# A gated graph network on one core: the first layer's two products in the other order

## The chip, the cores and the metric

The kernel runs on one core of one Trainium2 chip. The core has TensorE (PE: matmuls, with its weight loads shown apart as PEld), VectorE (DVE), ScalarE (ACT), GpSimd (POOL) and SyncE (SP), which issues all DMA transfers of this kernel. The metric is the time of one execution in device microseconds, as the median of the runs.

## The reference

There are 128 graphs of 128 nodes with 256 features, and one adjacency matrix for all of them. A first layer computes `norm(x + adj x W0 + b0)`; a gated recurrent network with three steps follows, then a residual and another norm.

```python
y = jnp.einsum('nm,bmd->bnd', adj, x)                  # first layer
x = _layernorm(x + jnp.einsum('bnd,do->bno', y, weight) + bias)
h = x
for _ in range(3):
    a = jnp.einsum('nm,bmd->bnd', adj, h)              # in_mat = out_mat = adj
    av = jnp.concatenate([a, a], axis=-1)
    z = sigmoid(_lin(av, w3_w, w3_b) + _lin(h, u3_w, u3_b))
    r = sigmoid(_lin(av, w4_w, w4_b) + _lin(h, u3_w, u3_b))
    hv = jnp.tanh(_lin(av, w5_w, w5_b) + _lin(r * h, u5_w, u5_b))
    h = (1.0 - z) * h + z * hv
out = _layernorm(x + h)
```

All of it is float32.

## The kernel before

**Tiling.** Four graphs make a group (1024 float32 values in each of 128 partitions); there are 32 groups. One step of one group is a *slot*; there are 96 slots. `at(s)` says which group and step slot s is: four groups advance in turn, so of 12 slots the first four are step 0 of four groups, the next four step 1, the last four step 2. The DVE work differs: in slots s with s mod 12 from 1 to 8 the state just updated must be turned (`state_blocks`, L881); in s mod 12 = 9, 10, 11, 0 it is not. The text calls these *heavy* and *light* slots.

**Split products.** A float32 operand is split in a high part (an fp32r copy, made by ACT, `copy`) and a low part (full minus high, made by DVE, `low_part`, L745). A product is then three fp32r matmuls, hi·hi, lo·hi and hi·lo, that accumulate in PSUM. So every operand of PE costs one ACT and one DVE pass of 128x1024.

**A slot on PE** (L537 to L546): `graph(s+1)` (adjacency times the next slot's state, L447, 6 matmuls of 512 columns), `state_product(s)` (12, L379), then `first_layer(s)` if there is any, `r_product` (12), `candidate_product` (12), `gates` (24). The text takes the beginning of `graph(s+1)` as the beginning of slot s.

**The graph result's way.** The adjacency product is by nodes; the gates want features in the partitions. DVE turns 32x32 blocks of it (`graph_blocks`, L826, two operations of 512), SP writes them to DRAM (`write_a`) and reads them back with the quadrants exchanged (`read_a`, four DMAs), ACT makes `a_hi` from what landed and DVE `a_lo`. The same trip by DRAM is made by the state (`state_blocks`, `write_h`, `read_h`) and by the first layer's result (`first_blocks`, `write_h0`, `read_h0`).

**The first layer** of groups 4 to 31 is spread over the slots of earlier groups, one group per three slots, by `GRAPH, WEIGHTS, NORM = -12, -10, -9`. In a slot with s mod 3 = 0 PE does `first_graph` (L402: 8 float32 matmuls of 128 columns with x itself as the weights, which the profile counts as 16); ACT and DVE split the result (`ax_hi`, `ax_lo`). In the slot two later (s mod 3 = 2) PE does `first_weights` (L413: 24 matmuls of 256 columns) and DVE `first_sum` (L788, and statistics). In the next one (s mod 3 = 0 again) ACT does `first_norm` and DVE `first_blocks`. POOL adds the bias to x (`add_bias`, L1014) once `first_graph` is done, and computes scale and shift. An output group is finished in slots with s mod 3 = 1 (`residual` on DVE, L815, with statistics) and 2 (`result_norm` on ACT). The text speaks of slots of kind 0, 1 and 2, by s mod 3.

**Order.** There is no scheduler: each engine runs the loop `for s in range(END + 1)` in the order written, and waits on semaphores. What stands behind a waiting instruction on its engine waits too. Among the waits: `state_product(s+1)` needs both halves of z of slot s (`z_ready`), since they share PSUM banks; `gates(s)` ends with the `u5` product, which needs `rh_hi` (ACT) and `rh_lo` (DVE) of this slot.

Of the kernel before, what the change touches and what calls it, by code (L numbers as in the profile page):

```python
# [11 lines left out]
G = 4  # L12
C = 2
Q = 32
# [5 lines left out]
def gnn_kernel(nc, x, adj_t, w0, b0, w3_t, w4_t, w5_t, u3_t, u5_t, biases, out):  # L20
# [31 lines left out]
    def group_at(s, offset):  # L52

        g, rest = divmod(s - offset, STEPS)
        return g if rest == 0 and FOUR <= g < GROUPS else None

    def graph_at(s):

        return FOUR if s == 1 else group_at(s, GRAPH) if s > 0 else None
# [8 lines left out]
    GRAPH, WEIGHTS, NORM = -12, -10, -9  # L68
# [16 lines left out]
    with ExitStack() as ctx:  # L85
# [56 lines left out]
        h0_scratch = scratch("h0_scratch")  # L142
# [18 lines left out]
        def by_node(ps):  # L161
            return ps[:, :, :].rearrange("p c (b d) -> p (c b) d", d=D)

# [31 lines left out]
        x_half = sem("x_half")  # L195
        x_loaded, out_stored = some(X_RING, sem, "x_loaded"), some(2, sem, "out_stored")
# [44 lines left out]
        def _(sp):  # L241
# [70 lines left out]

            def store_last():
# [24 lines left out]
            load(4)  # L338

            for s in range(END + 1):  # L340
                h0_next = group_at(s, NORM + 1) if s + 1 >= FOUR else s + 1
# [29 lines left out]
        def _(pe):  # L371
# [13 lines left out]
            def first_graph(g, batches=range(G)):  # L385
# [7 lines left out]
                if g >= FOUR:  # L393
                    pe.wait_ge(y_added, after(g - 1))
# [11 lines left out]
            def first_weights(g, batches=range(G)):  # L406
                banks, (hi, lo) = first_banks(g), first_parts(g)
                pe.wait_ge(ax_lo_ready, after(g) if batches[-1] == G - 1 else 1)
                for b in batches:
                    for c in range(C):  # L410
                        cols = slice(b * N, (b + 1) * N)
                        for n, (v, w) in enumerate(((hi, w0_hi), (hi, w0_lo), (lo, w0_hi))):
                            mm = pe.matmul(by_node(banks)[:, b, :], v[:, c, cols], w[:, c, :],  # L413
                                           start=n == 0 and c == 0, stop=n == 2 and c == C - 1,
                                           skip_group_check=True)
                mm.then_inc(y_done, 1)
# [141 lines left out]
        def _(act):  # L558
# [9 lines left out]
            def first_graph_high(g):  # L568
                hi, _ = first_parts(g)
                act.wait_ge(ax_done, after(g))  # L570
                if g >= FOUR:
                    act.wait_ge(y_done, after(g - 1))
                elif g >= 2:
                    act.wait_ge(y_done, after(g - 2))
                copy(hi[:, :, :], first_banks(g)[:, :, :]).then_inc(ax_hi_ready, 1)

# [45 lines left out]
            def node_high(s):  # L622
# [12 lines left out]
                copy(in_quadrants(nat_hi), chunks_first(src)).then_inc(nat_hi_ready, 1)  # L635
# [74 lines left out]
            for s in range(END + 1):  # L710
# [6 lines left out]
                if (g := graph_at(s)) is not None:  # L717
                    first_graph_high(g)
# [18 lines left out]
                if s < SLOTS:  # L737
                    update_gate(s)
                    candidate(s, 0)


        @block.vector
        def _(dve):
# [39 lines left out]

            def first_sum(g):
# [7 lines left out]
            def first_blocks(g):  # L792
                dve.wait_ge(h0_ready, g + 1)
                if g >= 1:
                    dve.wait_ge(h0_written, g * 16)
                if g < FOUR:
# [23 lines left out]
            def graph_blocks(s):  # L820
# [4 lines left out]
                for c in range(C):  # L825
                    tr = dve.transpose(a_blocks[:, :, c, :].rearrange("p i (b e) -> p i b e", e=Q),  # L826
                                       ps_a[:, c, :].rearrange("p (i b f) -> p i b f", b=G, f=Q))
                tr.then_inc(a_blocks_ready, 1)

            def node_low(s):  # L830
# [3 lines left out]
                low_part(in_quadrants(nat_lo), chunks_first(src), in_quadrants(nat_hi)).then_inc(nat_lo_ready, 1)  # L834
# [126 lines left out]
            for s in range(END + 1):  # L961
# [26 lines left out]
                if (g := graph_at(s)) is not None:  # L988
# [14 lines left out]
        def _(pool):  # L1003
# [6 lines left out]
            def add_bias(g):  # L1010
                pool.wait_ge(ax_done, after(g))
# [48 lines left out]
            for s in range(END + 1):  # L1060
# [3 lines left out]
                if (g := graph_at(s)) is not None:  # L1064
                    add_bias(g)
                if (g := group_at(s, WEIGHTS)) is not None:
# [37 lines left out]
```

## Time and profile before

| | us |
|---|---|
| median of 3 runs | 1620.86 (1619.14 to 1620.9) |
| the profiled execution | 1620.69 |
| its span | 1618.9 |
| PE busy | 1599.5 (99%) |
| DVE busy | 1427.4 (88%) |
| ACT busy | 940.4 (58%) |
| POOL busy | 265.6 (16%) |
| DMA | 268.26 MB, queue busy 52.9% |

Busy time is the time in which at least one instruction of the engine ran. Matmuls overlap each other, so one matmul's duration says little; the chain of waits, in which each piece begins where the one before it ends, tells what a group of matmuls costs. TensorE's granted clock was full (1.00) in the stretches that are used below. In a timeline the bracket behind a row is the idle time ahead of it and who ended it.

### The profile page before, as it was taken

To read this page: it belongs to the slowest core of one execution; us is meant where nothing else is said; L and a number is where in the kernel's file an instruction comes from. 1 tells how busy PE (TensorE), PEld (TensorE's weight loads), DVE (VectorE), ACT (ScalarE), POOL (GpSimd) and SP (SyncE) were. 2 spreads that over 40 slices of the span, in tenths; PEclk is the share of its full clock that TensorE was granted. 3 is DMA by queue.
4 is the path that set the end of the run, shared out by engine and by line. 5 is a ranking of instruction groups with operands and counts; after the bars stand their busy time and mean duration, and the time that the engine had idled before them with its cause. 6 is when DMAs were issued, how large, how long until landed. Compare 5 with 4: busy or idle time off the path is not lost.

```text
span 1618.9 us, 21710 instructions
## 1 busy us (share of the span) xinstructions
PE 1599.5 (99%) x7684; PEld 1348.8 (83%) x7684; DVE 1427.4 (88%) x1904; ACT 940.4 (58%) x1364; POOL 265.6 (16%) x302
## 2 busy tenths in 40 slices
PE   8999999999999999999999999999999999999996
PEld 8888888888888888888888888888888888888875
DVE  6788888999889998998889988999988999888888
ACT  4556556565555666565665556565656555556554
POOL 5111111111111111101111111111011111100022
PEclk9999999999999999999999999999999999999998
DMA  5444345664456553666526664355644566556534
GB/s 158 140 157 147 127 140 173 196 204 151 127 169 208 185 168 104 183 207 196 169 102 185 191 212 144 125 187 176 214 143 136 178 195 183 156 146 201 177 127 143
DMA packets 195596, 268.26 MB, mean 166 GB/s; under 512 B 18976, under 2 KB 167456, under 8 KB 195488
## 3 DMA queue, kind: packets, MB, share of 16 engines
q1 hardware_dynamic: 195488, 266.88, 52.9%
q8 instruction: 61, 1.00, 0.3%
q14 instruction: 47, 0.39, 0.1%
HBM read 135.21 MB, written 131.60 MB: 165 GB/s over the span
## 4 chain that ended last, share of the span: by engine, by line
PE 93%; DVE 3%; DMA 1%; SPq 1%; ACT 0%; issue 0%; POOL 0%; ACTq 0%; DVEq 0%; POOLq 0%
PE ps_r L379 46%; PE ps_h L379 31%; PE ps_a L447 8%; PE ps_l L413 5%; PE ps_l L402 3%; SPq L259 1%; DMA bias_row<-b 0%; PE ps_a L428 0%; DMA h_scratch_a<-h_blocks_a 0%; DVE out_sums L750 0%; DVE a_blocks L826 0%; DVE nat_lo L745 0%; DVE hv L866 0%; DMA a_landed<-a_scratch_b 0%; DVE h_t_h L873 0%
## 5 line engine op out<-in xcount | busy, mean ns | idle before, releaser
L826 DVE STREAM_TRANSPOSE a_blocks<-ps_a 128x512 f32<-128x512 f32 x184 | 120.0, 690 | 81.8 <-PE ps_a L447 81.5
L666 ACT ACTIVATE rh<-ps_r,bias_r 128x512 f32<-128x512 f32 x192 | 131.1, 688 | 104.2 <-PE ps_r L379 100.8
L560 ACT ACTIVATE rh_hi<-rh 128x512 fp32r<-128x512 f32 x192 | 119.0, 633 | 107.2 <-DVE rh L854 106.6
L682 ACT ACTIVATE hv<-ps_h,bias_h 128x512 f32<-128x512 f32 x192 | 128.9, 686 | 43.1 <-PE ps_h L379 42.5
L1022 POOL TENSOR_TENSOR out_var_eps_sb<-out_meanvar,eps 128x4 f32<-128x4 f32 x31 | 7.4, 239 | 808.6 <-DVE out_meanvar L756 808.6
L745 DVE TENSOR_TENSOR rh_lo<-rh,rh_hi 128x512 fp32r<-128x512 f32 x192 | 125.8, 689 | 9.2
L866 DVE TENSOR_TENSOR hv<-hv,z_sb 128x1024 f32<-128x1024 f32 x95 | 116.5, 1226 | 11.0 <-DVE hv L863 1.4
L678 ACT ACTIVATE z_sb<-ps_r,bias_z 128x512 f32<-128x512 f32 x192 | 119.9, 672 | 4.4 <-PE ps_r L379 4.4
L560 ACT ACTIVATE nat_hi<-h_landed_a 128x1024 fp32r<-128x1024 f32 x39 | 41.4, 1062 | 139.4 <-DMA h_landed_a<-h_scratch_a 129.4
L379 PE MATMUL ps_h<-rh_hi,u_hi 128*128 128x512 f32 x384 | 119.1, 391 | 1.6 <-ACT rh_hi L560 1.5
L379 PE MATMUL ps_r<-a_hi_a,w_hi 128*128 128x512 f32 x384 | 119.9, 393 | 0.6 <-ACT rh L666 0.6
L379 PE MATMUL ps_r<-a_hi_b,w_hi 128*128 128x512 f32 x384 | 119.8, 393 | 0.0
L379 PE MATMUL ps_h<-rh_lo,u_hi 128*128 128x512 f32 x384 | 118.7, 390 | 0.0
L379 PE MATMUL ps_h<-rh_hi,u_lo 128*128 128x512 f32 x384 | 118.7, 390 | 0.0
L379 PE MATMUL ps_r<-h_hi,u_hi 128*128 128x512 f32 x384 | 118.5, 390 | 0.0
L379 PE MATMUL ps_r<-a_hi_a,w_lo 128*128 128x512 f32 x384 | 118.4, 389 | 0.0
L379 PE MATMUL ps_r<-a_hi_b,w_lo 128*128 128x512 f32 x384 | 118.4, 389 | 0.0
L379 PE MATMUL ps_r<-h_lo,u_hi 128*128 128x512 f32 x384 | 118.3, 389 | 0.0
L379 PE MATMUL ps_r<-a_lo_a,w_hi 128*128 128x512 f32 x384 | 118.3, 389 | 0.0
L379 PE MATMUL ps_r<-a_lo_b,w_hi 128*128 128x512 f32 x384 | 118.3, 389 | 0.0
L379 PE MATMUL ps_r<-h_hi,u_lo 128*128 128x512 f32 x384 | 118.2, 389 | 0.0
L379 PEld LDWEIGHTS ps_h<-rh_hi,u_hi 128*128 128x128 f32 x384 | 72.2, 188 | 17.3 <-ACT rh_hi L560 2.4
(291 smaller groups left out, 4006.6 us busy)
## 6 DMA issues: line engine op xcount, KB each, us to landing
h_scratch_a<-h_blocks_a SPq DMA_DIRECT2D x48, 512.0 KB, 5.3
h_landed_a<-h_scratch_a SPq DMA_DIRECT2D x192, 128.0 KB, 2.9
h_scratch_b<-h_blocks_b SPq DMA_DIRECT2D x47, 512.0 KB, 3.5
h_landed_b<-h_scratch_b SPq DMA_DIRECT2D x188, 128.0 KB, 2.9
a_scratch_a<-a_blocks SPq DMA_DIRECT2D x46, 512.0 KB, 2.6
a_landed<-a_scratch_a SPq DMA_DIRECT2D x184, 128.0 KB, 2.9
a_scratch_b<-a_blocks SPq DMA_DIRECT2D x46, 512.0 KB, 2.7
a_landed<-a_scratch_b SPq DMA_DIRECT2D x184, 128.0 KB, 2.8
```

What stands on the lines that cost most here:

```text
L259: sp.dma_start(landed[to * Q:(to + 1) * Q].rearrange("q i c x -> q i (c x)"), by_target[to]).then_inc(moved, 16)
L379: mm = pe.matmul(psum[:, o, :], w[:, c, o * P:(o + 1) * P], v[:, c, :], start=start and n == 0 and c == 0, stop=stop and n == 2 and c == C ...
L402: mm = pe.matmul(into, x_in[g % X_RING][:, b, c * P:(c + 1) * P], adjt[:, :], start=True, stop=True)
L413: mm = pe.matmul(by_node(banks)[:, b, :], v[:, c, cols], w[:, c, :], start=n == 0 and c == 0, stop=n == 2 and c == C - 1, skip_group_check ...
L447: mm = pe.matmul(ps_a[:, c, :], w[:, :], v[:, c, :], start=k == 0, stop=k == 2, skip_group_check=True)
L560: return act.activation(dst, src, ACT.Copy)
L666: act.activation(rh[:, c, :], ps_r[:, c, :], ACT.Sigmoid, bias=bias_r[:, c:c + 1]).then_inc(r_ready, 1)
L678: act.activation(z_sb[:, c, :], ps_r[:, c, :], ACT.Sigmoid, bias=bias_z[:, c:c + 1]).then_inc(z_ready, 1)
L682: act.activation(hv[:, c, :], ps_h[:, c, :], ACT.Tanh, bias=bias_h[:, c:c + 1]).then_inc(hv_ready, 1)
L745: return dve.tensor_tensor(dst, full, hi.bitcast(F32), ALU.subtract)
L826: tr = dve.transpose(a_blocks[:, :, c, :].rearrange("p i (b e) -> p i b e", e=Q), ps_a[:, c, :].rearrange("p (i b f) -> p i b f", b=G, f=Q))
L866: dve.tensor_tensor(hv[:, :, :], hv[:, :, :], z_sb[:, :, :], ALU.mult).then_inc(scaled_ready, 1)
```

## The change

**What PE computes.** For groups 4 to 31 the first layer is adjacency times (x W0) and no longer (adjacency times x) W0. `first_product(g)` is 24 fp32r matmuls of 256 columns with the turned x as weights, `graph_of_product(g)` 6 fp32r matmuls of 512 columns with the split adjacency as weights. Groups 0 to 3 stay as they were.

**How x is turned.** x W0 wants features in the partitions. DVE turns x in 32x32 blocks (`turn`), SP writes them to a new DRAM tensor (`write_x`) and reads them back into the buffer `h_t` of that group, which is free then (`read_x`). ACT and DVE split it (`turned_high`, `turned_low`) and split the product as well (`product_high`, `product_low`).

**When.** The table gives `TURN` = 3g-14 (kind 1), `PRODUCT` = 3g-11 (kind 1), `SUM` = 3g-10 (kind 2), `NORM` = 3g-9 (kind 0). Group 4 has numbers of its own. The load of x moves from kind 1 to kind 2, two slots ahead of `TURN`. POOL's `add_bias` waits for `turn` and no longer for PE.

**Graph result.** `nat_hi` and `nat_lo` are filled flat, in the order of their source, so that the graph result can be turned in one operation of 1024.

```diff
-    GRAPH, WEIGHTS, NORM = -12, -10, -9
+    LATER = range(FOUR, GROUPS)
+    TURN = {g: 0 if g == FOUR else STEPS * g - 14 for g in LATER}
+    PRODUCT = {g: 2 if g == FOUR else STEPS * g - 11 for g in LATER}
+    SUM = {g: PRODUCT[g] + 1 for g in LATER}
+    NORM = {g: PRODUCT[g] + 2 for g in LATER}
+    BLOCKS_AT = {g: 5 if g == FOUR else NORM[g] for g in LATER}
...
                 if FOUR <= s + 1 < SLOTS:
                     write_a(s + 1)
                 if h0_next is not None:
                     write_h0(h0_next)
+                if x_next is not None:
+                    write_x(x_next)
...
                     read_h0(h0_next)
+                if x_next is not None:
+                    read_x(x_next)
...
-                if (g := group_at(s, GRAPH - 2)) is not None and g > FOUR:
+                if (g := group_at(s, TURN, -2)) is not None and g >= FOUR + 2:
                     load(g)
...
+            def first_product(g):
+                pe.wait_ge(y_added, after(g - 1))
+                pe.wait_ge(xt_lo_ready, g - FOUR + 1)
...
+            def graph_of_product(g):
+                pe.wait_ge(xw_lo_ready, g - FOUR + 1)
+                for half in range(C):
+                    for k, (w, v) in enumerate(((adj_hi, ax_hi), (adj_lo, ax_hi), (adj_hi, ax_lo))):
+                        mm = pe.matmul(ps_l[:, half, :], w[:, :], v[:, half, :], start=k == 0, stop=k == 2,
...
             def first_layer(s):
-                if (g := graph_at(s)) is not None:
-                    first_graph(g)
-                if (g := group_at(s, WEIGHTS)) is not None:
-                    first_weights(g)
+                if (g := group_at(s, PRODUCT)) is not None:
+                    first_product(g)
+                if (g := group_at(s, SUM)) is not None:
+                    graph_of_product(g)
...
+            def turned_high(g):
+                act.wait_ge(y_done, after(g - 1))
+                act.wait_ge(x_moved, (g - FOUR + 1) * MOVED)
...
+            def product_high(g):
+                act.wait_ge(xw_done, g - FOUR + 1)
+                copy(flat(ax_hi), flat(ps_l)).then_inc(xw_hi_ready, 1)
...
-                for c in range(C):
-                    tr = dve.transpose(a_blocks[:, :, c, :].rearrange("p i (b e) -> p i b e", e=Q),
-                                       ps_a[:, c, :].rearrange("p (i b f) -> p i b f", b=G, f=Q))
+                tr = dve.transpose(flat_blocks(a_blocks).rearrange("p (x e) -> p x e", e=Q),
+                                   flat(ps_a).rearrange("p (x f) -> p x f", f=Q))
...
-                if (g := graph_at(s)) is not None:
-                    first_graph_low(g)
-                if (g := group_at(s, WEIGHTS)) is not None:
+                if (g := group_at(s, PRODUCT)) is not None:
+                    product_low(g)
+                if (g := group_at(s, SUM)) is not None:
                     first_sum(g)
-                if (g := group_at(s, NORM)) is not None:
+                if (g := group_at(s, BLOCKS_AT)) is not None:
                     first_blocks(g)
+                if (g := group_at(s, TURN)) is not None:
+                    turn(g)
+                if (g := group_at(s, PRODUCT, -1)) is not None:
+                    turned_low(g)
...
-                pool.wait_ge(ax_done, after(g))
+                if g < FOUR:
+                    pool.wait_ge(ax_done, after(g))
+                else:
+                    pool.wait_ge(x_blocks_ready, g - FOUR + 1)
```

POOL's order stays as it is: `first_scale` of one group (its last operation is `h_shift`, L1028), and then `add_bias` of the next. The names `ax_hi`, `ax_lo` serve the turned x and the product in turn. `h_blocks` stands for the buffers of the first layer (`h0_blocks`) and of the state alike. Three places where the order of instructions changes. DVE, slot 43 (kind 1), from the graph result's low part to the end; before:

```order
570 L745 TENSOR_TENSOR a_lo_a<-a_landed,a_hi_a 128x1024
571 L815 TENSOR_TENSOR h_nat_d<-h_nat_d,h_landed_b 128x1024
572 L750 BN_STATS out_sums<-h_nat_d 128x6 x4
573 L756 BN_AGGR out_meanvar<-out_sums 128x2 x4
574 L826 STREAM_TRANSPOSE a_blocks<-ps_a 128x4x128 x2
```

and of the changed kernel:

```order
599 L822 TENSOR_TENSOR a_lo_a<-a_landed,a_hi_a 128x1024
600 L822 TENSOR_TENSOR ax_lo<-ps_l,ax_hi 128x1024
601 L869 STREAM_TRANSPOSE h_blocks<-x_in_d 128x8x4x32
602 L918 TENSOR_TENSOR h_nat_d<-h_nat_d,h_landed_b 128x1024
603 L827 BN_STATS out_sums<-h_nat_d 128x6 x4
604 L833 BN_AGGR out_meanvar<-out_sums 128x2 x4
605 L930 STREAM_TRANSPOSE a_blocks<-ps_a 128x1024
```

Two operations, the product's low part and the turning of x, now stand between the graph result's low part and the residual, and the turning of the graph result is one operation. DVE, the end of slot 42 (kind 0), before:

```order
557 L745 TENSOR_TENSOR h_lo<-h_t_h,h_hi 128x1024
558 L745 TENSOR_TENSOR a_lo_b<-a_landed,a_hi_b 128x1024
559 L745 TENSOR_TENSOR ax_lo<-ps_l,ax_hi 128x1024
560 L802 STREAM_TRANSPOSE h_blocks<-h_nat_b 128x1024
561 L826 STREAM_TRANSPOSE a_blocks<-ps_a 128x4x128 x2
```

and of the changed kernel:

```order
586 L822 TENSOR_TENSOR h_lo<-h_t_h,h_hi 128x1024
587 L822 TENSOR_TENSOR a_lo_b<-a_landed,a_hi_b 128x1024
588 L905 STREAM_TRANSPOSE h_blocks<-h_nat_b 128x1024
589 L822 TENSOR_TENSOR ax_lo<-h_t_c,ax_hi 128x4x8x32
590 L930 STREAM_TRANSPOSE a_blocks<-ps_a 128x1024
```

Here the count stays: the low part of the graph product makes room for that of the turned x (`ax_lo<-h_t_c`). SP's DMA queue around a slot of kind 2, before:

```order
355 L259 DMA h_landed_a<-h_scratch_a 32x4x256 x4
356 L254 DMA a_scratch_a<-a_blocks 128x1024
357 L259 DMA a_landed<-a_scratch_a 32x4x256 x4
358 L254 DMA h_scratch_b<-h_blocks_b 128x1024
359 L259 DMA h_landed_b<-h_scratch_b 32x4x256 x4
```

and of the changed kernel:

```order
255 L283 DMA h_landed_a<-h_scratch_a 32x4x256 x4
256 L278 DMA a_scratch_a<-a_blocks 128x1024
257 L278 DMA x_scratch<-h_blocks 128x1024
258 L283 DMA a_landed<-a_scratch_a 32x4x256 x4
259 L283 DMA h_t_c<-x_scratch 32x4x256 x4
260 L275 DMA x_in_d<-x 128x4x256
261 L278 DMA h_scratch_b<-h_blocks_b 128x1024
262 L283 DMA h_landed_b<-h_scratch_b 32x4x256 x4
```

The write of x stands between the write and the read of the graph result, and the read of x and the load of another group ahead of the state's write.

## Rows read from the trace of the kernel before

**Rows 1.** The page: busy time and share of the span of each engine.

```profile
span 1618.9 us, 21710 instructions
PE 1599.5 (99%) x7684; PEld 1348.8 (83%) x7684; DVE 1427.4 (88%) x1904; ACT 940.4 (58%) x1364; POOL 265.6 (16%) x302
```

**Rows 2.** Waits of PE, the largest: for whom, us in total, times, longest.

```profile
PE ps_l L413 <- DVE nat_lo L745: 3.4, 1, 3.4
```

**Rows 3.** The chain of waits, slots 41 to 43: start, us, what.

```profile
710.26 1.36 PE ps_a L447 x6
...
714.34 2.87 PE ps_l L413 x24
...
728.12 1.36 PE ps_a L447 x6
...
732.20 1.78 PE ps_l L402 x16
...
744.88 1.36 PE ps_a L447 x6
```

**Rows 4.** Timeline of DVE, slots 40 to 43 and 45: start, us, operation.

```profile
708.47 1.23 DVE L745 TENSOR_TENSOR a_lo_b<-a_landed,a_hi_b 128x1024 fp32r<-128x1024 f32 x1 [0.65 <-ACT a_hi_b L560]
...
712.67 1.28 DVE L826 STREAM_TRANSPOSE a_blocks<-ps_a 128x512 f32<-128x512 f32 x2
...
729.52 1.31 DVE L826 STREAM_TRANSPOSE a_blocks<-ps_a 128x512 f32<-128x512 f32 x2 [1.23 <-PE ps_a L447]
...
734.56 1.25 DVE L881 STREAM_TRANSPOSE h_blocks_a<-h_t_f 128x1024 f32<-128x1024 f32 x1
735.73 1.20 DVE L881 STREAM_TRANSPOSE h_blocks_b<-h_t_d 128x1024 f32<-128x1024 f32 x1
736.86 1.18 DVE L745 TENSOR_TENSOR nat_lo<-h_landed_b,nat_hi 128x1024 fp32r<-128x1024 f32 x1
737.96 1.28 DVE L854 TENSOR_TENSOR rh<-rh,h_t_g 128x512 f32<-128x512 f32 x2
...
742.82 1.22 DVE L745 TENSOR_TENSOR ax_lo<-ps_l,ax_hi 128x1024 fp32r<-128x1024 f32 x1
743.96 1.24 DVE L802 STREAM_TRANSPOSE h_blocks<-h_nat_b 128x1024 f32<-128x1024 f32 x1
746.28 1.31 DVE L826 STREAM_TRANSPOSE a_blocks<-ps_a 128x512 f32<-128x512 f32 x2 [1.09 <-PE ps_a L447]
...
785.31 2.15 DVE L745 TENSOR_TENSOR nat_lo<-h_landed_b,nat_hi 128x1024 fp32r<-128x1024 f32 x1
```

**Rows 5.** Timeline of ACT, slots 40 to 44, the same columns.

```profile
722.91 1.06 ACT L560 ACTIVATE a_hi_a<-a_landed 128x1024 fp32r<-128x1024 f32 x1 [0.83 <-DMA a_landed<-a_scratch_a]
...
739.81 1.05 ACT L560 ACTIVATE a_hi_b<-a_landed 128x1024 fp32r<-128x1024 f32 x1
...
742.74 1.24 ACT L678 ACTIVATE z_sb<-ps_r,bias_z 128x512 f32<-128x512 f32 x2
...
757.31 1.06 ACT L560 ACTIVATE a_hi_a<-a_landed 128x1024 fp32r<-128x1024 f32 x1 [1.76 <-DMA a_landed<-a_scratch_a]
```

**Rows 6.** Timeline of POOL, slots 42 and 45.

```profile
730.01 0.20 POOL L1028 TENSOR_TENSOR h_shift<-h_mean_rstd,minus_one 128x4 f32<-128x4 f32 x1
...
781.66 1.24 POOL L1028 TENSOR_TENSOR h_shift<-h_mean_rstd,minus_one 128x4 f32<-128x4 f32 x1
783.65 2.72 POOL L1014 TENSOR_TENSOR x_in_d<-x_in_d,bias_row 128x1024 f32<-128x1024 f32 x1 [0.74 <-PE ps_l L402]
```

**Rows 7.** Timeline of SP's DMA queue, slot 44 (issues).

```profile
764.19 0.34 SPq L254 DMA_DIRECT2D a_scratch_b<-a_blocks  x1
769.27 1.73 SPq L259 DMA_DIRECT2D a_landed<-a_scratch_b  x4
```

**Rows 8.** Stretches: slots 40 and 41 (kinds 1, 2); the last columns are clock, DMA share, GB/s.

```profile
695.30:710.26 14.96, 14.96 (x68) 12.39 (x67) 12.96 (x15) 8.22 (x11) 0.00 (x0) 1.00 0.81 222
710.26:728.12 17.86, 17.86 (x92) 15.26 (x91) 17.21 (x30) 9.92 (x15) 3.38 (x4) 1.00 0.53 176
```

More of the change, by code:

```diff
@@ L50, in output_slot, with group_at, turned_in_a_blocks @@
         return slot_of(g, STEPS - 1) + 1 + (0 if g >= GROUPS - FOUR else 2 * (g % FOUR))
[L52 to L59, printed above, removed]
+    LATER = range(FOUR, GROUPS)
[4 more added lines that the diff above has]
+    BLOCKS_AT = {g: 5 if g == FOUR else NORM[g] for g in LATER}
+    def group_at(s, stage, behind=0):
+        for g in LATER:
+            if stage[g] + behind == s:
+                return g
+        return None
+    def turned_in_a_blocks(g):
+        return g < FOUR + 2
     def after(g):
@@ L338, in _ @@
             load(4)
+            load(5)
             for s in range(END + 1):
-                h0_next = group_at(s, NORM + 1) if s + 1 >= FOUR else s + 1
+                h0_next = group_at(s, BLOCKS_AT, 1) if s + 1 >= FOUR else s + 1
+                x_next = group_at(s, TURN, 1)
                 if FOUR <= s + 1 < SLOTS:
@@ L415, in first_weights @@
                                            skip_group_check=True)
+                mm.then_inc(y_done, 1)
+            def first_product(g):
+                pe.wait_ge(y_added, after(g - 1))
+                pe.wait_ge(xt_lo_ready, g - FOUR + 1)
+                hi, lo = by_batch_and_chunk(ax_hi), by_batch_and_chunk(ax_lo)
+                for b in range(G):
+                    for c in range(C):
+                        for n, (v, w) in enumerate(((hi, w0_hi), (hi, w0_lo), (lo, w0_hi))):
+                            mm = pe.matmul(by_node(ps_l)[:, b, :], v[:, b * C + c, :], w[:, c, :],
+                                           start=n == 0 and c == 0, stop=n == 2 and c == C - 1,
+                                           skip_group_check=True)
+                mm.then_inc(xw_done, 1)
+            def graph_of_product(g):
[3 more added lines that the diff above has]
+                        mm = pe.matmul(ps_l[:, half, :], w[:, :], v[:, half, :], start=k == 0, stop=k == 2,
+                                       skip_group_check=True)
                 mm.then_inc(y_done, 1)
@@ L716, in _ @@
                     state_high(s + 1)
-                if (g := graph_at(s)) is not None:
-                    first_graph_high(g)
+                if (g := group_at(s, PRODUCT, -1)) is not None and g > FOUR:
+                    turned_high(g)
+                if (g := group_at(s, PRODUCT)) is not None:
+                    product_high(g)
                 if s < SLOTS:
@@ L782, in first_graph_low, with turn, turned_low, product_low @@
                 low_part(lo[:, :, :], first_banks(g)[:, :, :], hi[:, :, :]).then_inc(ax_lo_ready, 1)
+            def turn(g):
+                dve.wait_ge(x_loaded[g % X_RING], (g // X_RING + 1) * 16)
+                into = flat_blocks(a_blocks) if turned_in_a_blocks(g) else h0_blocks[:, :, :].rearrange("p i x -> p (i x)")
+                earlier = [k for k in LATER if k < g and turned_in_a_blocks(k) == turned_in_a_blocks(g)]
+                if earlier:
+                    dve.wait_ge(x_written, (earlier[-1] - FOUR + 1) * 16)
+                if not turned_in_a_blocks(g):
+                    dve.wait_ge(h0_written, 16 * (FOUR + len([k for k in LATER if BLOCKS_AT[k] < TURN[g]])))
+                dve.transpose(into.rearrange("p (i r e) -> p r i e", i=BLOCKS, e=Q),
+                              x_in[g % X_RING][:, :, :].rearrange("p b (c i f) -> p (b c) i f", c=C, f=Q)
+                              ).then_inc(x_blocks_ready, 1)
+            def turned_low(g):
+                dve.wait_ge(xt_hi_ready, g - FOUR + 1)
+                parts = (by_batch_and_chunk(t).rearrange("p r (j e) -> p j r e", e=Q) for t in (ax_lo, ax_hi))
+                lo, hi = parts
+                low_part(lo, h_t[g % H_RING][:, :, :, :].rearrange("p j c (b e) -> p j (c b) e", e=Q),
+                         hi).then_inc(xt_lo_ready, 1)
+            def product_low(g):
+                dve.wait_ge(xw_hi_ready, g - FOUR + 1)
+                low_part(flat(ax_lo), flat(ps_l), flat(ax_hi)).then_inc(xw_lo_ready, 1)
             def first_sum(g):
@@ L795, in first_blocks @@
                     dve.wait_ge(h0_written, g * 16)
+                if g >= FOUR:
+                    turned = [k for k in LATER if TURN[k] < BLOCKS_AT[g]]
+                    dve.wait_ge(x_written, len(turned) * 16)
                 if g < FOUR:
@@ L833, in node_low @@
                 dve.wait_ge(nat_hi_ready, n + 1)
[L834 removed]
+                low_part(flat(nat_lo), flat_blocks(src), flat(nat_hi)).then_inc(nat_lo_ready, 1)
             def state_low(s):
```

43 lines of the change are left out of this document (33 added, 10 removed).

## The prediction

> **What bounds the kernel now.** Read first the page's busy times: PE is busy for 99% of the span, DVE for 88%, ACT for 58% [rows 1]. A matmul's busy time overlaps the next one's, so 99% alone doesn't prove a bound. The waits of PE do: the largest is one of 3.4 us in the ramp, before the steady state [rows 2]. After that the chain of waits is PE piece after PE piece without a gap [rows 3]. So what PE has to do sets the time, and three slots take 49.58 us (slots 40 to 42: 744.88 minus 695.30; the first stretch begins there [rows 3, 8]). The third thing to read is how near the others are. In these three slots DVE idles ahead of three operations, 0.65 + 1.23 + 1.09 = 2.97 us [rows 4]. That is all the room that it has in heavy slots.
>
> The profiled execution took 1620.69 us, 1618.9 of span and 1.8 around it; the median of the runs is 1620.86. The sum is made against 1620.7.
>
> **PE's part: 0.42 us per group less.** The pass of x by the adjacency costs 1.78 us (8 float32 matmuls, counted as 16) [rows 3]. It goes. The 24 matmuls with W0 cost 2.87 us [rows 3] and stay, with another operand as weights. The new pass by the split adjacency is six matmuls of 512 columns, the same form as the state's graph pass, 1.36 us [rows 3]. 1.78 - 1.36 = 0.42 us, times 28 groups = 11.8 us. If nothing else moved, the time would be 1620.7 - 11.8 = 1608.9. The three slots of a group would last 49.16 us. They are divided otherwise than before: kind 1 now has the 2.87 (14.96 + 2.87 = 17.83 us), kind 2 the 1.36 (16.32), and kind 0 has nothing any more (14.96, where slot 42 had 16.76).
>
> **DVE's part: 2.1 us per group more.** Added is one turning of 1024 (in rows 4 the next operation begins 735.73 - 734.56 = 1.17 us after) and one more low part (743.96 - 742.82 = 1.14). The graph result's two operations take 1.24 us (1.31 less the overlap with the next), one of 1024 should take the 1.17 of the other turnings: 0.07 us less in each slot, 0.21 per group. 1.17 + 1.14 - 0.21 = 2.1 us. The DVE work of three heavy slots was 49.58 - 2.97 = 46.6 us and becomes 48.7, against 49.16 of PE. It still fits, by 0.45 us; but only if DVE never waits for anybody. No row shows a low part in pieces of 32 elements, as the turned x has them. The turnings all work in such pieces and take 1.20 to 1.25 us, as long as the other forms of 1024 [rows 4], so I take nothing for it; the bounds are nothing and 0.1 us, the spread between the forms.
>
> **Other parts.** ACT gets one more pass of about 1.05 us [rows 5] per group, at 58% busy, in kind 1, between state_high and the reset gate; there PE does the product first, so it costs nothing. If that cover went, it would be 1.0 us. SP gets five more DMAs per group and 1 MB of traffic. The DMA engines were 81% busy at 222 GB/s in kind 1, which makes 274 GB/s at most, and 53% busy in kind 2, 176 GB/s x 17.86 us = 3.1 MB [rows 8]. The write and the read of x come into kind 2, and the load of x moves there: three times 0.5 MB more, 4.7 MB in 16.3 us or 288 GB/s. That is more than they carry, so part of it will run on into kind 0. In the ramp (groups 4 to 6) DVE has no residual to do; I take the 0.42 us there in full.
>
> **Where it doesn't fit: kind 0.** Take slot 42, which began at 728.12. DVE turned the graph result at +1.40, began `rh` at +9.84 [rows 4]; ACT began `a_hi` at +11.69 and ended z at 743.98, +15.86 [rows 5]. PE needs z for the next state product, at 744.88 + 1.36, which is +18.12. That was 2.3 us of slack. Without the pass of x by the adjacency, PE is there at 14.96 + 1.36 = +16.32, and the slack is 0.5 us. The same holds for the end of the slot (`rh_hi` for the u5 product): it also loses the 1.78 us. Two things eat the 0.5.
>
> First, how late DVE comes into the slot. Kind 1: DVE enters it about 1.1 us late, since in kind 0 it is ready at 745.19 - 728.12 = +17.1 (1.09 before 746.28), plus 0.4 for the port below, and PE's graph pass is ready at +16.4. The graph result's trip by DRAM, from the turning to `a_hi`, took 757.31 - 746.28 = 11.0 us in slot 43 and 722.91 - 712.67 = 10.2 in slot 41 [rows 4, 5], and DVE waits for it in both. In kind 1 then: 1.4 + 1.1 + 11.0 = 13.5, ACT's pass 1.1, the low part and the residual 712.67 - 708.47 = 4.2 us [rows 4], the two added operations 2.3: DVE is free at 21.1, and PE's next graph result at 17.83 + 1.40 = 19.2. So it enters kind 2 late by 1.9. Kind 2: 1.4 + 1.9 + 10.2 + 1.1 + 4.3 (low part and `first_sum`, which has as many operations) = 18.9 against 16.32 + 1.40 = 17.7. It enters kind 0 late by 1.2 us. The 10.2 may change. SP issued the graph's write in slot 41 late, behind the state's read, and that goes, since the slot before is longer now; but the write of x runs beside it. In slot 44 a write beside another transfer took 769.27 - 764.19 = 5.1 us until SP could read it back [rows 7]. I take 0.3 us less in all, and 0.9 us of lateness; bounds are 0 (the trip 1.2 us shorter, by the SP delay alone) and 2.5 (the write of x costs its share of a full queue, 1.3 us more).
>
> Second, POOL. `add_bias` takes 2.7 us and in slot 45 began at 783.65 and ended at 786.37; DVE's `nat_lo`, begun at 785.31, took 2.15 us where it takes 1.18 otherwise [rows 4, 6]: it stood until POOL was done. So far `add_bias` waited for PE and fell on the turnings, which are not held up. Now it follows `h_shift` at once. When DVE comes late, POOL's small operations wait for DVE's updates (`h_shift` 1.24 us in slot 45 against 0.20 in slot 42 [rows 6]), and `add_bias` gets in behind the third update; 2.7 us then cover the two turnings (2.3 us) and hold `nat_lo` by 0.4 us. The Trainium skill, SBUF — State Buffer, Who interferes with whom, says that a DVE instruction with two SBUF inputs and a GpSimd instruction that reads SBUF contend for one port pair and that the order of issue decides who blocks. The 2.15 us of slot 45 agree with it. That is the third rival below.
>
> Sum for one group: 0.9 + 0.4 - 0.5 = 0.8 us that PE waits in kind 0. The groups with all the work are 7 to 31 (the residual begins in slot 10): 25 x 0.8 = 20 us. 1620.7 - 11.8 + 20 = 1628.9. I forecast 1629, slower by 0.5%. Its own range is 1623 to 1640.
>
> **The rivals.** (1) *PE's gain comes through.* DVE enters kind 0 late by no more than 0.1 us, and PE waits nowhere: 1608.9; with 0.2 us of waits per group 1614. For it: the work of 48.7 fits in 49.16, light slots have 1.17 us less, and the trip of kind 2 loses SP's delay. Against it: three places must each go well. (2) *The loop is simply DVE's.* PE waits as much as it gained, 0.42 us in each group, because DVE and the two DRAM trips already set about 49.6 us: 1621. (3) *POOL takes the port first.* If DVE has idle time at the beginning of kind 0, as the 1.23 us in slot 42 [rows 4], then `h_shift` is done at 730.21 [rows 6], before the first update at 730.8, and `add_bias` holds the updates until 732.9: 2.2 us. PE then waits 2.2 - 0.5 = 1.7 us. In all 25 groups this is 42 us, 1651; in the six light ones, with 1.17 us more slack, 3 us, and it is in every case's range. The point from which it decides is about 0.3 us of DVE idle time there. Note that this speaks against rival 1: a DVE that is early is punished by POOL, one that is late by z. (4) *The full queue.* The lateness into kind 0 is 2.5 us, PE waits 2.4 us in the 19 groups in heavy slots: 1608.9 + 46 = 1655.
>
> **Chances.** Forecast 0.41; rival 1 0.27; rival 2 0.19; rival 3 0.05; rival 4 0.08. Within 0.2%, which is about what a measurement of this kernel can tell from no change, lies 1617.6 to 1624.1: rival 2 and the lowest part of the forecast. So faster 0.28, same 0.20, slower 0.52. The range 1609 to 1650 leaves out most of rivals 3 and 4, and times below the full gain.
>
> **What would show it.** Right or wrong step by step: PE's chain should show six matmuls of 1.36 us in kind 2 and 2.87 us in kind 1; if they cost more, the gain is wrong. One turning of the graph result should read about 1.2 us. PE's waits should be on z or `rh_hi` in kind 0, about 0.8 us in each of 25 groups; if they are on `a_lo` or `xw_lo`, the place is wrong. The trip to `a_hi` should read 10 to 11 us in kinds 1 and 2. `x_in` on POOL should begin right behind `h_shift`, and a DVE operation beside it should read over 2 us. The prediction is wrong if PE has no waits and the span is 12 us shorter, or if one wait is of another kind than these.

## The result and the profile after

The changed kernel takes 1656.43 us (median of 5 runs, 1654.61 to 1660.02), the one before 1619.83 us beside it (5 runs, 1618.94 to 1620.9). The ratio is 1.0224, with a 95% interval of 1.0212 to 1.0236: slower by 36.6 us, where 1629 was forecast and 1609 to 1650 given as range. The direction was right; the loss came out more than four times as large as the 8.3 us (1629 against 1620.7) that were forecast.

The page of the changed kernel, first the busy times, then two groups of section 5 (busy, mean ns | idle ahead of it and who ended it):

```profile
span 1654.4 us, 21361 instructions
PE 1609.1 (97%) x7404; PEld 1324.3 (80%) x7404; DVE 1527.3 (92%) x1868; ACT 961.0 (58%) x1392; POOL 282.6 (17%) x302
DVE 42%; PE 29%; DMA 9%; issue 8%; SPq 7%; ACT 4%; POOL 0%; DVEq 0%; ACTq 0%; POOLq 0%
L625 ACT ACTIVATE rh_hi<-rh 128x512 fp32r<-128x512 f32 x192 | 119.1, 631 | 156.1 <-DVE rh L958 156.0
L930 DVE STREAM_TRANSPOSE a_blocks<-ps_a 128x1024 f32<-128x1024 f32 x92 | 113.4, 1233 | 27.9 <-PE ps_a L512 27.6
```

PE was busy for 99% of the span and DVE for 88% [rows 1]; now it is 97 and 92. The third row is the chain that ended last, by engine: it now runs over DVE more than over PE. DVE was busy for 1427.4 us and is for 1527.3, that is 100 us more, where the forecast's 2.1 us for each of 28 groups make 59. So about 40 us of DVE time are there that no added operation explains. DVE also waits little for PE: 27.9 us in all ahead of the turned graph result.

The chain of waits through one slot of kind 0 (slot 39) and the two slots behind it (start, us, what) answers to [rows 3]:

```profile
694.89 1.13 DVE a_blocks L930
...
697.23 1.24 DVE hv L970
698.47 0.02 issue
698.49 3.48 DVE h_t_g L977
...
704.37 1.11 DVE nat_lo L822
705.47 0.62 DVE rh L958
...
706.11 1.24 ACT rh_hi L625 x2
...
707.39 2.77 PE ps_h L424 x11
710.17 1.36 PE ps_a L512 x6
711.53 2.97 PE ps_r L424 x12
714.50 2.87 PE ps_l L469 x24
...
732.36 1.36 PE ps_l L479 x6
```

The lower part is PE's, as forecast: the product with W0 costs 2.87 us, now in kind 1, and the new pass of x 1.36 us in kind 2. The upper part is not: in kind 0 DVE's queue alone sets the end, through its third update (`h_t_g`, 3.48 us), and PE waits for `rh_hi` at the end of the slot.

DVE's timeline there, and again one group later (the bracket is idle time ahead), answers to [rows 4]:

```profile
694.80 1.22 DVE L930 STREAM_TRANSPOSE a_blocks<-ps_a 128x1024 f32<-128x1024 f32 x1
695.95 1.18 DVE L967 TENSOR_TENSOR hv<-hv,h_t_g 128x1024 f32<-128x1024 f32 x1
697.23 1.23 DVE L970 TENSOR_TENSOR hv<-hv,z_sb 128x1024 f32<-128x1024 f32 x1
698.49 3.47 DVE L977 TENSOR_TENSOR h_t_g<-hv,h_t_g 128x1024 f32<-128x1024 f32 x1
...
712.57 1.24 DVE L930 STREAM_TRANSPOSE a_blocks<-ps_a 128x1024 f32<-128x1024 f32 x1
...
730.55 1.22 DVE L930 STREAM_TRANSPOSE a_blocks<-ps_a 128x1024 f32<-128x1024 f32 x1
...
746.00 1.25 DVE L930 STREAM_TRANSPOSE a_blocks<-ps_a 128x1024 f32<-128x1024 f32 x1 [0.22 <-PE ps_a L512]
...
749.72 3.46 DVE L977 TENSOR_TENSOR h_t_f<-hv,h_t_f 128x1024 f32<-128x1024 f32 x1
```

POOL's timeline, which answers to [rows 6]:

```profile
697.27 1.25 POOL L1139 TENSOR_TENSOR h_shift<-h_mean_rstd,minus_one 128x4 f32<-128x4 f32 x1
698.47 2.40 POOL L1125 TENSOR_TENSOR x_in_b<-x_in_b,bias_row 128x1024 f32<-128x1024 f32 x1
...
749.70 2.40 POOL L1125 TENSOR_TENSOR x_in_c<-x_in_c,bias_row 128x1024 f32<-128x1024 f32 x1
```

Read the two together. `h_shift` (128x4) stands from 697.27 until DVE's second update ends at 698.46. `add_bias` follows it at 698.47, and DVE's third update begins at 698.49 but lasts 3.47 us instead of 1.23. POOL's operation ends at 700.87 and the update at 701.96, 1.09 us later: it did nearly all of its work behind POOL's, and lost 2.24 us. This text calls such a loss a *hold*. Two starts 0.02 us apart would prove little about the order; that POOL's operation keeps its 2.40 us while DVE's grows does. One group later the starts are 749.70 and 749.72. From one turned graph result to the one three slots later it is 746.00 - 694.80 = 51.2 us, where it was 49.6 and PE's work is 49.16.

In the whole trace 22 third updates take over 3 us, and 7 first or second updates over 2.7. One of the 22, in slot 92, stands in the trace of before too and has nothing to do with `add_bias`. In slots 12 to 81 each of the 24 slots of kind 0 has one held update. It is the third in 20 slots, where DVE was idle for at most 0.22 us ahead of the turned graph result; it is the second in slots 48 and 72 and the first in 12 and 24, where DVE was idle for 0.64 to 1.39 us. In the trace of before no update of these slots is held, but 16 `nat_lo` take over 2.1 us, as the one in [rows 4]: there `add_bias` cost DVE about 1 us, and kind 0 had 2.3 us to spare.

Slot lengths, each from the start of its graph pass on PE to the next one's (means over slots 10 to 84, 25 of each kind):

| | PE's work alone | after | more, x 25 |
|---|---|---|---|
| kind 0 | 14.96 | 16.6 (heavy 17.15, light 16.11) | 41 us |
| kind 1 | 17.86 | 18.06 | 5 us |
| kind 2 | 16.32 | 16.34 | 0 |

Slots 10 to 84 took 1237.7 us before and take 1275.4 now; PE's work alone would be 1228.5 us. The loss is 47 us over PE's work, 41 of it in kind 0.

### The profile page after: what moved, and what is told of

Read it like the earlier page. It is cut to its first block, busy times and chain, and to the rows that moved or that the text cites. A ratio compares the mean times of both kernels' runs of the same rounds, so it can differ in the third digit from the quotient of the medians.

```text
span 1654.4 us, 21361 instructions
## 1 busy us (share of the span) xinstructions
PE 1609.1 (97%) x7404; PEld 1324.3 (80%) x7404; DVE 1527.3 (92%) x1868; ACT 961.0 (58%) x1392; POOL 282.6 (17%) x302
## 4 chain that ended last, share of the span: by engine, by line
DVE 42%; PE 29%; DMA 9%; issue 8%; SPq 7%; ACT 4%; POOL 0%; DVEq 0%; ACTq 0%; POOLq 0%
PE ps_r L424 13%; PE ps_h L424 10%; SPq L283 6%; DVE a_blocks L930 5%; DVE hv L970 3%; DVE hv L967 3%; DMA a_landed<-a_scratch_a 3%; DVE nat_lo L822 3%; DVE rh_lo L822 3%; PE ps_a L512 3%; DVE ax_lo L822 3%; DVE h_blocks_b L985 3%; ACT rh_hi L625 2%; DVE out_sums L827 2%; PE ps_l L469 2%
## 5 line engine op out<-in xcount | busy, mean ns | idle before, releaser
L424 PE MATMUL ps_h<-rh_hi,u_hi 128*128 128x512 f32 x384 | 127.8, 403 | 19.4 <-ACT rh_hi L625 17.0
L930 DVE STREAM_TRANSPOSE a_blocks<-ps_a 128x1024 f32<-128x1024 f32 x92 | 113.4, 1233 | 27.9 <-PE ps_a L512 27.6
L970 DVE TENSOR_TENSOR hv<-hv,z_sb 128x1024 f32<-128x1024 f32 x95 | 122.5, 1289 | 10.6 <-DVE hv L967 0.9
L424 PE MATMUL ps_r<-h_hi,u_hi 128*128 128x512 f32 x384 | 122.0, 399 | 1.1 <-ACT z_sb L751 1.1
L424 PEld LDWEIGHTS ps_h<-rh_hi,u_hi 128*128 128x128 f32 x384 | 72.3, 188 | 50.3 <-ACT rh_hi L625 36.6
L424 PEld LDWEIGHTS ps_r<-a_hi_b,w_hi 128*128 128x128 f32 x384 | 70.7, 189 | 23.5 <-ACT rh L739 10.1
```

The lines of the kernel that those rows point to most:

```text
L424: mm = pe.matmul(psum[:, o, :], w[:, c, o * P:(o + 1) * P], v[:, c, :], start=start and n == 0 and c == 0, stop=stop and n == 2 and c == C ...
L930: tr = dve.transpose(flat_blocks(a_blocks).rearrange("p (x e) -> p x e", e=Q), flat(ps_a).rearrange("p (x f) -> p x f", f=Q))
L970: dve.tensor_tensor(hv[:, :, :], hv[:, :, :], z_sb[:, :, :], ALU.mult).then_inc(scaled_ready, 1)
```

## The experiments

All are compared with the kernel before on the same chip: 1620.67 us beside the first four (31 runs), 1620.59 us beside the last four (15 runs). "Slots 10 to 84" is the stretch of the table above, from each one's trace, which is that of a single execution: 1622.13, 1619.54, 1620.92, 1620.88, 1609.97, 1617.4, 1609.41 and 1637.52 us for experiments 1 to 8. The one of experiment 3 is the longest of its ten, 4 us over its median; those of experiments 5 and 8 are the shortest of theirs.

**1. The bias behind the third update.** The changed kernel, with a wait in POOL's `add_bias` for groups 4 and later:

```
                     pool.wait_ge(x_blocks_ready, g - FOUR + 1)
+                    pool.wait_ge(h_ready, PRODUCT[g] - 1)
```

> Changed kernel, but POOL's add_bias of groups 4 to 31 also waits for the third update of DVE (h_ready) of its slot of kind 0, so that it falls on the two turnings. Theory (port): the update that took 3.47 us takes 1.23 again, nat_lo is held by 0.1 to 0.4 us at most; a group of three slots falls from 51.2 us to PE's 49.2, 25 to 28 groups give back 40 to 50 us: 1608 to 1618. Rival (DVE has too much work, or its DRAM trips are too long in the full queue): the time stays above 1640, PE still waits in kind 0.

1621.85 us (1620.82 to 1624.48, 10 runs), ratio 1.0009 [1.0, 1.0019]; slots 10 to 84 take 1241.7 us. DVE and then POOL of this kernel in the same slot:

```profile
683.58 1.23 DVE L970 TENSOR_TENSOR hv<-hv,z_sb 128x1024 f32<-128x1024 f32 x1
684.84 1.23 DVE L977 TENSOR_TENSOR h_t_g<-hv,h_t_g 128x1024 f32<-128x1024 f32 x1
...
688.40 1.32 DVE L822 TENSOR_TENSOR nat_lo<-h_landed_b,nat_hi 128x1024 fp32r<-128x1024 f32 x1
```

```profile
683.62 1.25 POOL L1140 TENSOR_TENSOR h_shift<-h_mean_rstd,minus_one 128x4 f32<-128x4 f32 x1
686.21 2.43 POOL L1126 TENSOR_TENSOR x_in_b<-x_in_b,bias_row 128x1024 f32<-128x1024 f32 x1 [1.35 <-DVE h_t_g L977]
```

One wait takes 34.6 us away, with every operation and DMA of the change still there. `add_bias` now runs beside the two turnings, which keep their 1.25 and 1.20 us. That is a heavy slot, where `nat_lo` is held by 0.14 us. In the 13 light slots of kind 0, with one turning, `add_bias` outlasts it and `nat_lo` takes 2.33 to 2.56 us in 12 of them (slots 12 to 81), a hold of 1.2 to 1.4 us where 0.1 to 0.4 at most were expected. The time was 4 us above what was expected at most, so something was left.

**2. The bias with the product.** Instead of that wait:

```
+                    pool.wait_ge(xw_done, g - FOUR + 1)
```

> Changed kernel, but add_bias also waits for PE's product of x and W0 (kind 1, 7 us into the slot), where DVE turns the state and makes nat_lo. Theory (port): nat_lo or rh of kind 1 is held by up to 2 us, part of it hidden by DVE's wait for the reset gate there; 1610 to 1635. Rival (too much work on DVE): above 1640.

1618.79 us (1615.82 to 1622.33, 10 runs), ratio 0.9989 [0.9979, 0.9998]; slots 10 to 84: 1240.7. The hold is not gone but moved to kind 1, where DVE's `nat_lo` takes it in 18 of the 25 slots (it lasts 2.28 to 3.04 us) and `rh` in the other seven (0.5 us in six of them):

```profile
704.91 2.29 DVE L822 TENSOR_TENSOR nat_lo<-h_landed_a,nat_hi 128x1024 fp32r<-128x1024 f32 x1
```

PE has 2.9 us more work in kind 1 than in kind 0, and kind 1 lasts 17.89 us there, 0.03 over PE's work: the hold has room. So what counts is where the hold falls, and with the hold out of kind 0 two different waits give nearly the same time.

**3. Nearly no bias.** `add_bias` works on 4 of the 1024 elements for groups 4 and later:

```
+                else:
+                    pool.tensor_tensor(x_in[g % X_RING][:, 0, 0:4], x_in[g % X_RING][:, 0, 0:4],
+                                       bias_row[:, 0:4], ALU.add).then_inc(x_biased, 1)
```

> Changed kernel with add_bias of groups 4 to 31 cut to 4 of 1024 elements (so the first layer's bias is left out for the rest): all waits and all other work stay. Theory (port): no DVE operation is held; 1607 to 1613, the 1609 that PE's work alone gives. Rival (too much work or too full a queue): above 1640. A mix would land between and say how much each has.

1616.83 us (1612.95 to 1620.92, 10 runs), ratio 0.9976 [0.9965, 0.9987]. The time was 4 us above the expected range. Without any hold by the bias 8 us over PE's 1608.9 remain; the largest waits of PE in this kernel:

```profile
PE ps_r L424 <- ACT rh L739: 8.2, 10, 2.7
PE ps_l L456 <- DVE nat_lo L822: 2.9, 1, 2.9
```

Five of the ten waits of the first row fall in slots 10 to 84, four of them in slots of kind 0 with s mod 12 = 9 and one in slot 66. The six slots with s mod 12 = 9 last 8.6 us longer than PE's work together; slot 69 is the worst, with 4.6 us. What SP's queue issued ahead of it:

```profile
1165.91 1.80 SPq L283 DMA_DIRECT2D h_t_d<-x_scratch  x4
1167.76 0.43 SPq L275 DMA_DIRECT2D x_in_a<-x  x1
1168.29 0.45 SPq L278 DMA_DIRECT2D h_scratch_b<-h_blocks_b  x1
1175.61 1.74 SPq L283 DMA_DIRECT2D h_landed_b<-h_scratch_b  x4
```

and what ACT waited for then:

```profile
1181.82 1.06 ACT L625 ACTIVATE nat_hi<-h_landed_b 128x1024 fp32r<-128x1024 f32 x1 [7.34 <-DMA h_landed_b<-h_scratch_b]
```

and the chain of waits around it, which runs through this write and read until PE's `gates`:

```profile
1168.29 7.31 DMA h_scratch_b<-h_blocks_b
...
1176.92 4.82 DMA h_landed_b<-h_scratch_b
...
1185.40 4.60 PE ps_r L424 x12
```

The state's write is issued behind the read of x and the load of the next x, 1 MB together, and can be read back only 7.3 us later. ACT stands 7.34 us for it, and the reset gate and `rh` stand behind ACT's `nat_hi`. Slot 69 is the extreme. In the six slots with s mod 12 = 8 the median from the write to the read-back is 6.7 us, against 3.4 in the kernel before, and the write itself is issued 11.2 to 12.9 us into the slot.

**4. The kernel before with one turning.** Before, with the graph result turned in one operation of 1024 (and the state's high and low part read flat), without the rest of the change:

```
-                for c in range(C):
-                    tr = dve.transpose(a_blocks[:, :, c, :].rearrange(...), ps_a[:, c, :].rearrange(...))
+                tr = dve.transpose(flat_blocks(a_blocks).rearrange("p (x e) -> p x e", e=Q),
+                                   flat(ps_a).rearrange("p (x f) -> p x f", f=Q))
```

> Kernel before with one part of the change alone: nat_hi and nat_lo filled flat, the graph result turned in one operation of 1024. Each slot gives DVE back 0.07 us, 6 us in all, none of it on PE's chain: both theories 1619 to 1621, no change. If it moves by more than 3 us, the form of the copies matters and not the count.

1620.03 us (1618.12 to 1622.71, 10 runs), ratio 1.0 [0.999, 1.0009]; slots 10 to 84: 1237.8, as before. This part of the change moves nothing by itself.

**5. The state's trip first, bias with the product.** Experiment 2, with SP's order changed in each slot: the read of x and the load of x move behind the state's write and read, and so behind the store of a result too.

```
-                if x_next is not None:
-                    read_x(x_next)
                 if h0_next in first_state:
                     read_h0_again(h0_next)
                 for g in output_at(s, STORE):
                     store(g)
-                if (g := group_at(s, TURN, -2)) is not None and g >= FOUR + 2:
-                    load(g)
                 if 1 <= s <= SLOTS and at(s - 1)[1] < STEPS - 1:
                     write_h(nth_move[at(s - 1)])
                     read_h(nth_move[at(s - 1)])
+                if x_next is not None:
+                    read_x(x_next)
+                if (g := group_at(s, TURN, -2)) is not None and g >= FOUR + 2:
+                    load(g)
```

> Changed kernel with add_bias waiting for PE's product (as in the run before), and with SP's order in kind 2 changed: the state's write and read now stand ahead of the read of x and of the load of x. Theory (the rest of the loss is the state's trip, stuck behind x in the queue, so that nat_hi and ACT are late in slots of kind 0): PE's waits in kind 0 go, 1618.8 falls to 1609 to 1614. Rival (the rest is DVE's work): no change, 1617 to 1620.

**1611.25 us** (1609.97 to 1612.87, 5 runs), ratio 0.9943 [0.993, 0.9955]. Slots 10 to 84 take 1232.0 us against 1228.5 of PE's work. SP's queue and then the largest waits of PE:

```profile
715.81 0.34 SPq L278 DMA_DIRECT2D h_scratch_b<-h_blocks_b  x1
718.96 1.73 SPq L283 DMA_DIRECT2D h_landed_b<-h_scratch_b  x4
720.78 1.80 SPq L283 DMA_DIRECT2D h_t_c<-x_scratch  x4
722.63 0.43 SPq L275 DMA_DIRECT2D x_in_d<-x  x1
```

```profile
PE ps_l L456 <- DVE nat_lo L822: 2.1, 1, 2.1
PE ps_h L424 <- ACT rh_hi L625: 2.0, 3, 1.4
```

Here, in slot 41, the state is read back 3.15 us after its write was issued. In the six slots with s mod 12 = 8 it is 3.3 us (median), and the write is issued 9.2 to 10.4 us into the slot, about 2 us sooner. The six slots behind them are within 0.1 us of PE's work in sum, where in experiment 2 they were 8.3 us over it. The order is worth 7.5 us. It is the fastest of the complete kernels: 0.57% faster than before, and 45 us faster than the change as it was made, with the same arithmetic.

**6. The state's trip first, bias behind the update.** Experiment 1 with the same order of SP.

> The same order of SP's queue, with add_bias behind DVE's third update in kind 0. Theory: 1621.9 falls by 4 to 9 us, to 1613 to 1618; what stays is the tenth or more by which add_bias holds nat_lo in slots with one turning. Rival (DVE's work): stays at 1620 to 1623.

1617.75 us (1616.18 to 1620.39, 11 runs), ratio 0.9984 [0.9976, 0.9993]; slots 10 to 84: 1238.8. The order is worth 4 us here. Between this kernel and experiment 5 lie 6.5 us, and only the place of `add_bias` differs. Of the 6.8 us by which slots 10 to 84 differ, 4.8 lie in light slots of kind 0, where `nat_lo` is held by up to 1.4 us, and nearly all of it in four of them (21, 33, 60 and 81). The heavy slots of kind 0 show no difference, and 2.2 us lie in kind 1. That the hold makes these four late, and the others not, was not tested by a run of its own.

**7. Neither bias nor the trip of x.** Experiment 3, and x's write to and read from DRAM left out for groups 8 to 31 (the other operations stay, on old data):

```
-                if x_next is not None:
+                if x_next is not None and x_next < H_RING:
                     write_x(x_next)
...
-                if x_next is not None:
+                if x_next is not None and x_next < H_RING:
                     read_x(x_next)
```

For these groups ACT's `turned_high` waits for DVE's turning of x and no longer for the read.

> Changed kernel with add_bias cut to 4 of 1024 elements for groups 4 to 31, and for groups 8 to 31 the write and the read of x by DRAM left out as well (the product then takes what lies in the buffer; DVE's and ACT's work on it stays, in count and size). Theory (queue): PE never waits in the steady state, 1616.8 falls to 1607 to 1610, what PE's work alone gives. Rival (DVE's work of 48.7 us in 49.2): 1614 to 1617.

1610.8 us (1609.28 to 1613.77, 4 runs), ratio 0.9942 [0.9928, 0.9955]; slots 10 to 84: 1231.2. That is 0.8 us above the expected range and 3 us below the rival's. DVE does all its added work here and PE is within 2 us of its 1608.9. So DVE's work is no bound (rival 2), and the order of experiment 5 gets back as much as leaving the trip out does (1611.25 against 1610.8, with ranges that overlap). One reading of experiment 3 needs care by it: the state's write takes 6.3 us (median of the same six slots) until it can be read back here too, with only the load of x, 0.5 MB, issued ahead of it. But it is issued 9.0 to 10.4 us into the slot, and the six slots behind it last 0.2 us over PE's work in sum. So what cost time was the whole trip, with the write both issued late and served late; served late alone, as here, it cost next to nothing.

**8. The kernel before with a second port user.** Before, with one more POOL operation (two SBUF inputs, an output that nobody reads) right behind `h_shift`; `add_bias` stays where it was:

```
                     first_scale(g)
+                    if g < LAST:
+                        pool.tensor_tensor(shadow[:, :, :], bias_row[:, :].unsqueeze(1).to_broadcast([P, G, D]),
+                                           bias_row[:, :].unsqueeze(1).to_broadcast([P, G, D]), ALU.add)
```

> Kernel before with one more POOL operation of 1024 elements with two inputs in SBUF (its result is not used) right behind h_shift, where the changed kernel has add_bias; add_bias itself stays behind PE's pass. Theory (port): a DVE update in kind 0 takes 3.4 us instead of 1.2 here too, in most groups; since z has 2.3 us of slack in kind 0 and DVE 3.0 us of idle time in three slots, PE waits little: 1620 to 1632, so most of the 36 us need both the hold and the shorter slot. Rival (the hold alone costs its 2.2 us times 25): 1670 or more.

1641.1 us (1637.52 to 1643.17, 4 runs), ratio 1.013 [1.0115, 1.0146]; slots 10 to 84: 1254.3, 16.6 more than before. Slot 42, DVE and then POOL:

```profile
737.90 2.68 DVE L864 TENSOR_TENSOR hv<-hv,h_t_f 128x1024 f32<-128x1024 f32 x1
740.68 1.23 DVE L867 TENSOR_TENSOR hv<-hv,z_sb 128x1024 f32<-128x1024 f32 x1
741.94 3.30 DVE L874 TENSOR_TENSOR h_t_f<-hv,h_t_f 128x1024 f32<-128x1024 f32 x1
```

```profile
737.60 1.90 POOL L1070 TENSOR_TENSOR shadow<-bias_row 128x1024 bf16<-128x1024 f32 x1
741.21 2.95 POOL L1015 TENSOR_TENSOR x_in_c<-x_in_c,bias_row 128x1024 f32<-128x1024 f32 x1 [1.71 <-PE ps_l L403]
```

The added operation holds the first update by 1.5 us, and the update chain, so shifted, then meets `add_bias`, which holds the third by 2.1: 3.6 us against 2.3 of slack. In the trace all 27 third updates of kind 0 from slot 3 to 81 are held (2.95 to 3.31 us), and in 18 of these slots a first or second one as well. I had reckoned with one hold, so the time came out 9 us over the expected range. It shows that holds alone, without any part of the change, make a loss of this kind (20.5 us) in the kernel before. It also shows that a hold is not a fixed price: it moves what comes behind it into the next one.

## Why the prediction was right and wrong

*PE's part: right.* 1.36 for 1.78 us, 2.87 us for W0 moved to kind 1, kind 0 with 14.96: all as said. With the bias and SP's order mended, 9.3 of the 11.8 us arrive (1620.6 to 1611.25).

*DVE's part: right in its work.* One turning takes 1.23 us where the two took 1.31 together, the low part from 32-element pieces 1.18, and the 48.7 us fit into 49.16 when nobody holds DVE (experiment 7). The changed kernel's other 40 us of DVE time are holds: held updates add 61 us to the lengths of DVE's operations, and 15 us of held `nat_lo` are gone.

*The slack of 0.5 us in kind 0: right in place.* PE's waits are on `rh_hi` and on the gates there. Heavy slots that DVE entered on time and with the third update held (27, 42, 54, 75, 78) last 16.79 to 16.82 us, 1.84 over PE's work: the hold of 2.24 less 0.4 of slack. The lost slack is also why an `add_bias` that cost PE nothing before is not free any more.

*First, the lateness by the DRAM trip: the place was right, the size too large.* The forecast took 1.1 us of lateness into kind 1, 1.9 into kind 2 and 0.9 into kind 0. In slots 39 and 42 the turned graph result began 1.9 and 1.4 us after the slot did, 1.4 being on time. The means over slots 12 to 83 are 0.94, 1.56 and 0.44 us, and none of kind 0 was over 2.0. The trip in kind 2 was 9.1 us (730.55 to `a_hi` at 739.63), where 9.9 was reckoned. ACT's rows in kinds 1 and 2, which answer to [rows 5]:

```profile
723.00 1.06 ACT L625 ACTIVATE a_hi_b<-a_landed 128x1024 fp32r<-128x1024 f32 x1 [0.76 <-DMA a_landed<-a_scratch_b]
...
739.63 1.05 ACT L625 ACTIVATE a_hi_a<-a_landed 128x1024 fp32r<-128x1024 f32 x1
```

The stretches of slots 39 to 41 (kinds 0, 1, 2), which answer to [rows 8]:

```profile
692.90:710.17 17.27, 15.95 (x68) 12.35 (x67) 16.86 (x22) 9.42 (x16) 5.67 (x5) 1.00 0.57 187
710.17:728.28 18.11, 18.11 (x91) 15.18 (x91) 17.45 (x18) 11.09 (x16) 0.00 (x0) 1.00 0.79 225
728.28:744.60 16.32, 16.32 (x73) 13.51 (x73) 15.88 (x25) 10.07 (x15) 3.31 (x4) 1.00 0.69 213
```

Kind 2 moved 213 GB/s with the DMA engines 69% busy, not the 288 that were reckoned. The engines were not full, and in this slot x's traffic did not run on as the prediction said: the last part of x's read landed at 742.24 and the load at 743.67, ahead of the slot's end at 744.60. What came late was the state's write, issued behind them at 738.68 and landed at 744.91. The prediction put no price on it; it was worth 4 to 7.5 us (experiments 5 and 6).

*Second, POOL: this step failed.* The forecast had `add_bias` get in behind the third update and hold `nat_lo` by 0.4 us. In 20 of the 24 slots of kind 0 from 12 to 81 it got in 0.02 us ahead of the third update and held it by 2.24 us; in the other four it held the first or the second by 1.6 to 2.2. The prediction had seen that `h_shift` waits for DVE's updates and drew the wrong end from it. POOL waits for the gap between two updates, and once it has that gap its next instruction is there first, since nothing stands between the two any more. So lateness does not keep `add_bias` behind the updates; it ties it to the gap. With the wait that the forecast had assumed (experiment 1), the measured time is 1621.85, 13 us over PE's 1608.9 where the sum had 20. Without that wait it is 34.6 us more. The sum also took the 0.8 us of heavy slots for all 25, though by the definition ahead 13 of these slots are light; in experiment 1 kind 0 lasts 0.34 us over PE's work in the heavy and 0.52 in the light ones.

Rival 3 had the mechanism and the price of one hold, but a condition that was too narrow. It asked for a DVE that is idle by 0.3 us or more at the beginning of kind 0. That was so in four of the 24 slots, and there the first or second update was held, as it said; in the other 20 DVE was idle for at most 0.22 us, and the hold came all the same, on the third. With the condition it got a chance of 0.05.

That its 1651 lies near the measured time is partly luck. It took 1.7 us for all 25 groups and counted six light ones; of the 24 slots with a hold 12 are light. By its own prices, 1.7 in the heavy and 0.53 in the light ones, the sum is 27 us and the time 1636. The six light slots with s mod 12 = 0 (12 to 72) did last 0.53 us over PE's work on average. The six with s mod 12 = 9 lasted 2.0 us over it, but experiments 2 and 3 still lose 8.3 and 8.6 us in these six with no hold in kind 0: that is the state's trip, which rival 3 did not have. The heavy ones lasted 2.2 us longer, not 1.7, since DVE's lateness adds to the hold. Rival 4's number (1655) is near the time, for another reason: the lateness of 2.5 us did not occur.

Rival 1, PE's gain comes through, nearly holds once both causes of waiting are gone (1611.25 against its 1608.9 to 1614). Rival 2 (1621, DVE as the bound) falls by experiment 7.

What stays open: the last 2.4 us between experiment 5 and PE's 1608.9, of which most lies in slots 18 and 66 (2.0 of the 3.5 us over PE's work in slots 10 to 84), and how much of the 6.5 us between experiments 5 and 6 is held time.

## What to carry to other kernels

When an operation loses the wait that it had, look up what now decides its start, and what its engine's port is shared with there. An operation that cost PE nothing behind one wait cost 35 us without it, and one line took that cost away. Price a hold by the slack of the slot in which it falls, and after shortening one engine's slot count again what the others had hidden in it. In a DMA queue, put the transfer that is wanted soonest first: behind 1 MB for a later group the state's write was issued about 2 us later and could be read back after 6.7 us instead of 3.3 (medians of experiments 2 and 5).

## What the runs showed of the hardware

- A POOL operation that follows another without a wait wins against a DVE operation due at the same moment. `add_bias` began at 698.47 and 749.70, the DVE update at 698.49 and 749.72, and DVE took 3.47 and 3.46 us instead of 1.23. The update began in the record but ended only 1.09 us after POOL's operation. The Trainium skill, SBUF — State Buffer, Who interferes with whom, says that the order of issue decides; the runs agree.
- Small POOL operations (128x4) are held in the same way, by DVE's updates: `h_shift` takes 1.25 us beside the second update in slot 39 and 0.20 us where it meets none [rows 6]. So it ends in the gap between two updates, and brings the next POOL operation there.
- DVE's turnings (one SBUF input) beside the same `add_bias` kept their 1.25 and 1.20 us (experiment 1); `nat_lo` and the updates, with two SBUF inputs, did not.
- A single PE wait in the list can understate the slot's loss. In slot 39 PE's row for `rh_hi` has 1.15 us of idle time, while the slot is 17.27 - 14.96 = 2.3 us longer; part of the rest comes right behind that row. The second matmul began at 707.39, 0.60 us after the first, where two of this form follow each other by 0.23 us otherwise: ACT ended the second half of `rh_hi` at 707.34.
